# One-hot picks chunk by chunk, and two tiles in flight, in a recommender tower

## The reference

```python
e = jnp.stack([tbl_0[ids[:, 0]], ..., tbl_25[ids[:, 25]]], axis=1)
combined = jnp.concatenate([e, r_dense_x[:, None, :]], axis=1)
z = jnp.einsum('bfd,bgd->bfg', combined, combined)[:, _TRIU_I, _TRIU_J]
h = jnp.concatenate([z, r_dense_x], axis=1)
h = jnp.maximum(h @ W_top1 + b_top1, 0.0)
h = jnp.maximum(h @ W_top2 + b_top2, 0.0)
y = h @ W_top3
```

## Time and profile before

| | us |
|---|---|
| median of 3 runs | 109.20 (109.17 to 109.23) |
| the profiled execution | 109.18 |
| its span, first to last instruction | 107.4 |
| PE, DVE, ACT, POOL busy in it | 98.5, 79.8, 75.0, 66.3 |

### The profile page before, as it was taken

How to read it: one execution, slowest core, us unless ns; L and a number is a source line. 1 busy time by engine, 2 the same in 40 slices (tenths; PEclk the granted TensorE clock), 3 DMA queues, 4 the chain that set the end, 5 groups by cost and what they waited for, 6 DMA issues and landing times.

```text
span 107.4 us, 2605 instructions
## 1 busy us (share of the span) xinstructions
PE 98.5 (92%) x998; PEld 79.0 (74%) x998; DVE 79.8 (74%) x162; ACT 75.0 (70%) x149; POOL 66.3 (62%) x72
## 2 busy tenths in 40 slices
PE   5999899989799999999798978999999989998992
PEld 1356676657467675887478958999999979997991
DVE  6599999999999999999943974588338922685120
ACT  4499999999999999999706842475527732474430
POOL 3777777777777787777877777777777750000000
PEclk9999999999999999999999999999999999999999
DMA  3852749995663636621211221221121220000000
GB/s 46 334 209 58 235 76 372 374 345 113 217 197 101 221 78 218 225 92 49 55 49 49 53 50 49 63 66 49 49 55 49 58 67 3 6 0 0 6 0 1
DMA packets 5200, 11.64 MB, mean 108 GB/s; under 512 B 1979, under 2 KB 2491, under 8 KB 5189
## 3 DMA queue, kind: packets, MB, share of 16 engines
q1 hardware_dynamic: 3120, 7.27, 21.2%
q0 software_dynamic: 2048, 4.20, 14.2%
q10 hardware_dynamic: 20, 0.02, 0.1%
HBM read 11.48 MB, written 0.00 MB: 107 GB/s over the span
## 4 chain that ended last, share of the span: by engine, by line
DVE 46%; PE 44%; issue 6%; ACT 2%; POOL 0%; DVEq 0%; POOLq 0%
DVE onehot L464 22%; PE gram_ps L613 13%; DVE low L476 13%; PE top_ps L678 5%; PE tr_ps L594 5%; PE act_ps L667 4%; PE dve_ps L667 4%; DVE onehot L470 3%; DVE xt L473 2%; PE gram_ps L578 2%; PE top_ps L702 2%; PE tr_ps L653 1%; DVE xt L450 1%; PE dve_ps L626 1%; PE act_ps L626 1%
## 5 line engine op out<-in xcount | busy, mean ns | idle before, releaser
L287 POOL DMA_INDIRECT rows<-table,ids_sb x64 | 65.5, 1023 | 20.8 <-issue 19.2
L578 PE MATMUL gram_ps<-onehot,high 128*128 128x512 f32 x82 | 23.1, 410 | 1.9 <-DVE onehot L464 1.6
L578 PE MATMUL gram_ps<-onehot,low 128*128 128x512 f32 x82 | 22.1, 411 | 0.0
L578 PEld LDWEIGHTS gram_ps<-onehot,high 128*128 128x128 f32 x82 | 14.3, 188 | 8.8 <-DVE onehot L464 5.0
L578 PEld LDWEIGHTS gram_ps<-onehot,low 128*128 128x128 f32 x82 | 15.4, 189 | 3.9
L464 DVE TENSOR_TENSOR onehot<-dve_ps,row_f 128x1024 fp32r<-128x1024 f32 (+1 forms) x10 | 14.4, 1479 | 1.2 <-PE act_ps L554 1.2
L464 DVE TENSOR_TENSOR onehot<-gram_ps,row_f 128x1536 fp32r<-128x1536 f32 (+1 forms) x10 | 14.9, 1531 | 0.0
L613 PE MATMUL gram_ps<-xt 128*58 128x52 f32 x512 | 14.5, 217 | 0.3 <-issue 0.3
L483 DVE COPY gram_sb<-gram_ps 26x208 f32<-26x208 f32 x32 | 12.0, 376 | 3.6 <-PE gram_ps L613 2.4
L613 PEld LDWEIGHTS gram_ps<-xt 128*58 128x58 f32 x512 | 14.0, 133 | 0.9 <-issue 0.5
L385 ACT ACTIVATE onehot<-onehot 128x1344 fp32r<-128x1344 f32 (+1 forms) x10 | 14.3, 1426 | 0.0
(11 more groups left out here) (83 smaller groups left out, 111.7 us busy)
## 6 DMA issues: line engine op xcount, KB each, us to landing
table<-table SPq DMA_DIRECT2D x9, 512.0 KB, 3.6
rows<-table,ids_sb POOLq DMA_INDIRECT x64, 2.9
w1p_sb<-w_pairs SPq DMA_DIRECT2D x1, 768.0 KB
table<-table SPq DMA_DIRECT2D x1, 640.0 KB, 3.8
w_sb<-w SPq DMA_DIRECT2D x1, 512.0 KB
dense_sb<-dense SPq DMA_DIRECT2D x1, 256.0 KB, 5.1
w1d_sb<-w_dense SPq DMA_DIRECT2D x1, 256.0 KB
ids_sb<-ids SPq DMA_DIRECT2D x1, 52.0 KB, 2.0
```

The lines of the kernel that those rows point to most:

```text
L287: pool.indirect_dma_start(rows[:, t, s - 1, :], None, tables[f], bass.IndirectOffsetOnAxis(ids_sb[:, t, f:f + 1], 0)).then_inc(gathered[t] ...
L578: last = pe.matmul(pick_ps[b][:], weights[:, c, :], onehot[:, b, c, :], start=(c == 0 and part == 0), stop=(c == CHUNKS[o] - 1 and part == 1))
```

## The change

- **DVE's pick stage.** The one-hot chunks are made one at a time, in whole chunks: DVE has 6 of 8 in even fields, 5 in odd ones, and 7 of 10 in the last, ACT the rest. The chunks of field o+1 alternate with the four subtraction pieces of field o.
- **PE's pick stage.** The high matmuls of field o+1 alternate with the low ones of field o. `pick` is split into `pick_high` and `pick_low`.
- **Spreads.** `select` has its rows twice, from partition 0 and from partition 32, and the ids too; the two spread matmuls of a field read 10 rows each from different row groups. The first field has a small `first` of its own. The second copy of the ids is made by ACT.
- **Pad.** The pad of `xt` is zeroed before the fields: tile 0 on DVE, tile 1 on ACT, tiles 2 and 3 on POOL.
- **Banks.** Tiles 0 to 2 have four transposed banks of four slots; the last tile keeps five. All of tiles 0 and 1 is transposed before the first Gram products.
- **Tiles.** ACT's and DVE's loops are unrolled. The products of tile 1 follow those of tile 0 at once, before the transpose back of tile 0, which now also waits until the products of tile 1 are copied. The three PSUM banks go round over all tiles.
- **Tail.** The dense part of tile 3 comes first, the second layer of tile 2 is cut in two around `back_last(2)`.

```diff
+BANKS = [range(n, n + 4) for n in range(1, NG + 1, 4)]
+LAST_BANKS = BANKS[:-1] + [range(NG - 3, NG), range(NG, NG + 1)]
+BANK_SLOTS = [BANKS] * (TILES - 1) + [LAST_BANKS]
...
-DVE_CHUNKS = {8: ((0, 1), (2, 3, 4)), 10: ((0, 1, 2), (3, 4, 5))}
-SHARED_COLS = {8: 192, 10: 368}
+DVE_CHUNKS = [6 if o % 2 == 0 else 5 for o in range(NO - 1)] + [7]
+DVE_BEFORE = [sum(DVE_CHUNKS[:o]) for o in range(NO + 1)]
+SPREAD_AT = (0, 32)
...
+            for t in (2, 3):
+                pool.memset(xt[:, t, :, N_SLOTS:PAD], 0.0).then_inc(pad_zero, 1)
             pool.wait_ge(ids_in, 16)
...
             def onehots(o):
...
                 act.wait_ge(ids_spread, o + 1)
                 if o >= 2:
                     act.wait_ge(pick_done, o - 1)
-                for c in range(shared(o), CHUNKS[o]):
...
+                for c in range(DVE_CHUNKS[o], CHUNKS[o]):
+                    last = act.activation(onehot[:, o % 2, c], ids_ps_act[o % 2], ACT.Abs, bias=row_neg[:, c:c + 1])
                 last.then_inc(distance_ready, 1)
...
             act.activation(row_neg[:], row_f[:], ACT.Copy, scale=-1.0).then_inc(row_neg_ready, 1)
+            act.wait_ge(field_ids_in, 16)
+            act.wait_ge(ids16_zero, 1)
+            act.activation(field_ids16[SPREAD_AT[1]:SPREAD_ROWS], field_ids[:], ACT.Copy).then_inc(ids16_again, 1)
+            act.activation(xt[:, 1, :, N_SLOTS:PAD], zeros[:, 0:1].rearrange("d (p s) -> d p s", p=1
...
             for o in range(NO):
-                if o == NO - 1:
-                    transposed(0, (0, 1))
                 onehots(o)
                 if o >= 1:
                     picked(o - 1)
...
+                if o == NO - 2:
+                    transposed(0, (1,))
+                if o == NO - 1:
+                    transposed(0, (3,))
+            transposed(1, (1,))
             picked(NO - 1)
-            transposed(1, (0, 1))
+            transposed(1, (3,))
...
+            dve.wait_ge(ids_spread, 1)
+            onehots(0, range(DVE_CHUNKS[0]))
             for o in range(NO):
...
                 dve.wait_ge(high_ready, o + 1)
...
+                if o + 1 < NO:
+                    dve.wait_ge(ids_spread, o + 2)
+                for r, piece in enumerate(rest_pieces(o)):
+                    rest(o, piece)
+                    if o + 1 < NO:
+                        if r == 0 and o >= 1:
+                            dve.wait_ge(pick_done, o)
+                        onehots(o + 1, (r,))
+                if o + 1 < NO:
+                    onehots(o + 1, range(REST, DVE_CHUNKS[o + 1]))
+                if o == NO - 3:
+                    transposed(0, (0,))
+                if o == NO - 2:
+                    transposed(0, (2,))
...
             gram(0)
-            dve.wait_ge(weights_in, WEIGHTS)
             squares(1)
             pack(1)
+            gram(1)
             back(1)
-            transposed(1, range(2, NT))
+            transposed(2, (0,))
+            squares(2)
+            pack(2)
+            dve.wait_ge(weights_in, WEIGHTS)
             first_layer(1)
...
+            def pick_high(o, chunks):
...
+                for c in chunks:
+                    if c == 0:
+                        if o >= 2:
+                            pe.wait_ge(pick_out, o - 1)
+                        pe.wait_ge(high_ready, o + 1)
+                    if c < DVE_CHUNKS[o]:
+                        pe.wait_ge(onehot_dve, DVE_BEFORE[o] + c + 1)
+                    elif c == DVE_CHUNKS[o]:
+                        pe.wait_ge(onehot_act, o + 1)
...
+            def pick_low(o, r):
...
+                pe.wait_ge(low_ready, REST * o + r + 1)
...
+                if r == REST - 1:
                     last.then_inc(pick_done, 1)
...
             def back(t):
 
+                pe.wait_ge(gram_out_act, max(t + 1, 2) * SETS)
+                pe.wait_ge(gram_out_dve, max(t + 1, 2) * SETS)
...
-            for o in range(NO - 1):
-                pick(o, 0)
+            pe.wait_ge(select_ready, 1)
+            spread(1)
+            pick_high(0, range(CHUNKS[0]))
+            for o in range(NO):
                 if o + 2 < NO:
                     spread(o + 2)
-                pick(o, 1)
...
+                for r in range(REST):
+                    pick_low(o, r)
+                    if o + 1 < NO:
+                        pick_high(o + 1, (r,))
+                if o + 1 < NO:
+                    pick_high(o + 1, range(REST, CHUNKS[o + 1]))
...
+                if o == NO - 4:
+                    transposes(0, (0, 1))
+                if o == NO - 3:
+                    transposes(0, (2, 3))
+                if o == NO - 2:
+                    transposes(1, (0, 1))
+            transposes(1, (2, 3))
...
             gram(0)
...
+            pe.wait_ge(weights_in, WEIGHTS)
+            dense_part(0, (0, 1))
+            gram(1)
+            transposes(2, (0, 1))
+            back(0)
+            dense_part(0, (2, 3))
+            first_layer(0, range(N1 // P))
+            transposes(2, (2,))
+            dense_part(1)
+            second_layer(0)
+            back(1)
+            transposes(2, (3,))
+            third_layer(0)
+            first_layer(1, range(N1 // P))
+            gram(2)
...
+            gram(3)
+            dense_part(3, (0, 2, 1, 3))
+            second_layer(2, (0,))
+            back_last(2)
+            second_layer(2, (1,))
+            back_last(1)
+            back_last(0)
```

More of the change, by code:

```diff
@@ new lines, in onehots, with rest @@
+            def onehots(o, chunks):
+                for c in chunks:
+                    dve.tensor_tensor(onehot[:, o % 2, c], ids_ps_dve[o % 2][:], row_f[:, c:c + 1].to_broadcast([P, B]),
+                                      ALU.is_equal).then_inc(onehot_dve, 1)
+            def rest(o, piece):
+                b = o % 2
+                dve.tensor_tensor(low[:, b, piece], table[:, o % TABLES, piece], high[:, b, piece].bitcast(F32),
+                                  ALU.subtract).then_inc(low_ready, 1)
@@ L555, in spread @@
                 last.then_inc(ids_spread, 1)
-            def pick(o, part):
+            def pick_high(o, chunks):
                 b = o % 2
-                if part == 0:
-                    if o >= 2:
-                        pe.wait_ge(pick_out, o - 1)
-                    pe.wait_ge(high_ready, o + 1)
-                    weights = high[:, b]
-                else:
-                    weights = low[:, b]
-                for c in range(CHUNKS[o]):
-                    if part == 0:
-                        if c < shared(o):
-                            made = [c in cs for cs in DVE_CHUNKS[CHUNKS[o]]].index(True) + 1
-                        else:
-                            made = DVE_PARTS
-                            pe.wait_ge(onehot_act, o + 1)
-                        pe.wait_ge(onehot_dve, DVE_PARTS * o + made)
-                    elif c in [piece.start for piece in rest_pieces(o)]:
-                        pe.wait_ge(low_ready, REST * o + [piece.start for piece in rest_pieces(o)].index(c) + 1)
-                    last = pe.matmul(pick_ps[b][:], weights[:, c, :], onehot[:, b, c, :],
-                                     start=(c == 0 and part == 0), stop=(c == CHUNKS[o] - 1 and part == 1))
-                if part == 1:
@@ new lines, in pick_high @@
+                for c in chunks:
+                    if c == 0:
[6 more added lines that the diff above has]
+                        pe.wait_ge(onehot_act, o + 1)
+                    pe.matmul(pick_ps[b][:], high[:, b, c, :], onehot[:, b, c, :], start=(c == 0), stop=False,
+                              skip_group_check=True)
@@ L581, in pick @@
+            def pick_low(o, r):
+                b = o % 2
+                pe.wait_ge(low_ready, REST * o + r + 1)
+                piece = rest_pieces(o)[r]
+                for c in range(piece.start, piece.stop):
+                    last = pe.matmul(pick_ps[b][:], low[:, b, c, :], onehot[:, b, c, :], start=False,
+                                     stop=(c == CHUNKS[o] - 1), skip_group_check=True)
+                if r == REST - 1:
                     last.then_inc(pick_done, 1)
@@ L675, in second_layer @@
                 pe.wait_ge(h1_out_dve, 2 * t + 2)
-                for m in range(N2 // P):
+                for m in parts:
                     for c in range(N1 // P):
```

246 lines of the change are left out of this document (105 added, 141 removed).

## The result

The changed kernel took 123.62 us (122.36 to 124.63), the one before 109.19: a ratio of 1.128 (1.121 to 1.135). The ratio is formed without the slowest of the four executions (124.63), the median with it. The profiled execution took 122.36, with a span of 120.5. Forecast were 119.3, in a range of 114 to 123.

What follows compares the result with a forecast made beforehand. DVE's and ACT's work per field was taken to bound the pick stage, PE the rest. The pick stage loses 12.2 us, middle and tail return 1.4 and 0.7: 109.2 + 10.1 = 119.3 us, range 114 to 123.

Steps and rivals of the forecast that it cites:

- the chain: Pick stage: pick o waits for field o+1's high copy; 5.65 or 6.23 us a field, average 5.94 against 4.5.
- The 0.10 for a weight load that can't hide: PE, each field: first weight load after a wait is exposed, taken as 0.10 us, between 0 and 0.23.
- The wait for the dense transposes: Turn 2: ACT waits for dense transposes on PE behind five high matmuls, until 20.5, then copies dense twice, 1.43 us.
- the table of field 2: Its load, released at 11.7, lands after 3.4 to 5.1 us, at 15.1 to 16.8; ACT would be ready at 15.2.
- the special turns 8 and 9: Last two picks: 7.2 us with a bank copy and ten-chunk high copy, then 4.9 us, ending at 68.8.
- Rival (C): PE's clock falls to 1.2 GHz: nine matmuls cost 2.1 us more, +16 over eight turns, 135 us; chance 0.03.
- S(2) - S(1): Time between ACT being able to read finished picks 1 and 2, forecast at 18.9 and 27.3 us.
- the start: Up to pick 0: spread 0.47 us later, ACT starts at 4.92 instead of 4.45, pick 0 readable at 13.2, before 11.9.
- the tile stage: From the first Gram products to the end: 1.4 us back in its middle part and 0.7 at its end.
- The tail: After the last Gram products: earlier dense part and half a second layer filling a wait give -0.7 us, ends 0 and -1.2.
- The middle: Tile stage: transposes moved ahead and a closed PE hole, less waits for DVE, give -1.4 us, ends 0 and -2.1.
- The bounds listed: Upward: weight loads +1.0, table landing +1.6, start +0.4, middle and tail +2.1, matmul and ACT steps 1.4 us.

Runs made afterwards that it cites:

- the first run above: Changed kernel with PE's pick order alone put back: four low pieces of a field, then all high chunks of the next; median 112.52 us (111.15 to 113.30).

## Why the prediction failed where it did

**Right: the chain.** Copy, distances, high copy, nine matmuls: 5.65 and 6.23 forecast, 5.55 and 6.13 measured. From the copy of pick 0 to that of pick 9 the sum was 68.8 - 13.2 = 55.6; with all gaps filled and the clock held up it is 69.08 - 14.61 = 54.5. The 0.10 for a weight load that can't hide was not there: nine matmuls take 2.36 from the wait, as from a full queue. The wait for the dense transposes, the table of field 2 and the special turns 8 and 9 were within 0.2 each.

**Wrong: the clock,** up to 3.2 us of the 4.3 that the median lies above the forecast. The sum had PE at the upper level throughout and put nothing for it. Rival (C) had the mechanism but was priced as all or nothing: +16 with the clock low in all eight turns, at 0.03. I held PE's share over a whole period (69%) against that of the tail (70%, clock 0.98). The falls stood behind single gaps: 1.7 us in a field, and 3.34 in turn 2, which my own sum implied (S(2) - S(1) = 8.4, with some 4.5 us of work for PE in it) and which I didn't look at. In the tail no gap of that length occurs; its clock after was 1.00 at 6.37 of 8.50 us. Filling a gap also raises PE's share, so the runs don't separate the length of a gap from the share around it. The Trainium skill (TensorE: Matmul & The Clock Gate, HAM oscillation — how this bites in real kernels) describes a kernel in which PE waits for transfers in every turn and starts the next one cold. Here the waits were for ACT, and only some turns started cold: the runs show falls behind gaps of 1.7 us, at changing places, and other gaps of that length without one.

**Wrong: the start,** +1.4 us. The prediction has the two pad memsets on POOL "lie in its wait for the ids, with at most 1 us of delay": that was asked of the wrong engine. They held up DVE's cast by 1.34 us, so the copy of pick 0 started at 14.6 to 14.7 instead of 13.2. With the memsets moved away it started at 13.13, so the rest of the start's sum was right. The length of the warm-up is a term that the sum lacked: 2.6 to 4.5 us in the traces, 4.00 and 2.87 in two kernels with the same code up to there. Its cause stays open. The Trainium skill (SBUF — State Buffer, Who interferes with whom) says that GpSimd and some VectorE copies and casts share one pair of ports as an exclusive lock, and the loser waits for the other instruction's end. The trace agrees that the cast waited for their end: it ended 0.03 us after the memsets. The cast's row starts at 1.23, ahead of the first memset's 1.39, and still it came last. I had looked up what a memset costs, not whom it blocks.

**Partly wrong: the tile stage.** Forecast 2.1 us back, measured 1.4. The tail gave 0.6 (0.7 forecast). The middle gave 0.8 of 1.4, of which 0.7 from the first to the third Gram start: 21.20 (72.21 to 93.41) against 21.89 (57.69 to 79.58); the closed hole was paid for with a wait for DVE's relu of the first layer ahead of the second dense part (0.85 us, where I had 0.5 for all waits around that layer).

With the clock held up the sum errs by +1.4 (start) - 1.1 (fields) + 0.7 (tile stage) = 1.0 us: 119.3 forecast, 120.38 measured.

**Wrong: the upper bound.** The bounds listed are +1.0, +1.6, +0.4, +2.1 and +1.4, together 6.5 us, so up to 125.8. The range stopped at 123, 2.8 us short of that, and no reason is given for the upper side. The measured median lies between the two. The start's bound of +0.4 was passed by 1.0, and the clock had none.

## What to carry to other kernels

When work of two steps is interleaved in one in-order queue, ask of each element in it what it waits for, and whether that lies behind the end of the very step that it now delays; the chain's sum, not any engine's load, is then the period. A gap on PE can cost more than its length where the clock follows, so a slower stage should be priced with its longest gaps too, not with its mean alone. And an instruction moved to an idle engine is free only if it doesn't hold up a busy one: two memsets on POOL ahead of the gathers made a cast on DVE 1.34 us later, and the kernel 1.35 us slower than with them on DVE (109.97 against 108.62). Before a difference between two kernels is put down to an edit, look where in the trace it arises: the 0.7 us that came with two moved memsets arose ahead of them, in the warm-up.

## What the runs showed of the hardware

- The granted clock fell behind some of PE's gaps of 1.7 us and more, in some executions and not in others, at different turns; behind gaps of 1.1 us in the pick stage no trace shows a fall. A fall cost 1.3 to 1.9 us between two copies of picks: 7.44 instead of 6.11 and 8.44 instead of 7.01 with turn 2 filled, 10.07 instead of 8.21 in the changed kernel. Zero matmuls in all gaps took away the falls and most of the scatter. Why the same gap was harmless in one execution and not in the next stays open.
- Ten matmuls of 512 columns in the warm-up took 2.6 to 4.5 us, while the granted clock is 1.00 from 4 to 9 us in every trace (2.61 in the kernel before, 4.47 in the first run above). So here that figure doesn't tell how fast PE runs.
- A POOL memset of 128 x 640 took 0.7 us; a DVE cast of 128 x 10 that starts at 1.23 in the profile ended 0.03 us after the second one, 1.34 us late.
- Spreads of 10 rows from two row groups run side by side: both start at 21.75, where before the second started 0.22 later. It didn't matter for the time, as PE was waiting anyway.
